# Masked attention scores in 64x32 instead of 64x64 tiles of the PE array

## The reference, cut to what matters

```
bq = q.reshape(b, h, w, WINDOW, d) * QK_SCALE          # 8 heads of 64, WINDOW = 64
bk, bv = (look_around(bk), look_around(bv))            # the window before and the window itself: 128 keys
sim = jnp.einsum('bhwid,bhwjd->bhwij', bq, bk)
mask = (i < j) | (i > j + WINDOW) | (j == -1)
sim = jnp.where(mask, -jnp.finfo(sim.dtype).max, sim)
attn = jax.nn.softmax(sim, axis=-1)
out = jnp.einsum('bhwij,bhwjd->bhwid', attn, bv)
```

## Time and profile before

| | |
|---|---|
| three executions, us | 430.07, 433.26, 432.17 (median 432.17) |
| profiled execution, us from first to last instruction | 428.4; its own device time is not listed apart, and the three lie 1.7 to 4.9 above it |
| PE busy | 406.9 us (95%) in 4851 matmuls |
| DVE, ACT, POOL busy | 339.0, 306.0, 289.0 us |
| local attention, first layer | about 90 to 222 us, second about 259 to 391 us |
| mean granted clock of PE | 0.998 |

### The profile page before, as it was taken

One profiled execution on the slowest core, in us unless ns is written; L12 is line 12 of the kernel. 1 busy time (PEld: TensorE's weight loads), 2 busy tenths in 40 slices (PEclk: granted clock), 3 DMA queues, 4 the chain that ended last, 5 costly groups with the idle time before them and its releaser, 6 DMA issues. The chain is left out here.

```text
span 428.4 us, 13218 instructions
## 1 busy us (share of the span) xinstructions
PE 406.9 (95%) x4851; PEld 290.3 (68%) x4851; DVE 339.0 (79%) x717; ACT 306.0 (71%) x690; POOL 289.0 (67%) x284
## 2 busy tenths in 40 slices
PE   5989999899999999999999999999999999999994
PEld 2667666557777777777776566677778777766563
DVE  4787777899798899899754376898899899855676
ACT  3868777777688878887873247688878878876324
POOL 2576799899778778777714346677777767761425
PEclk9999999999999999999999999999999999999999
DMA  7840000000000000000000000000000000000012
GB/s 194 311 98 2 4 3 3 2 1 2 13 10 9 12 10 8 8 16 8 6 8 15 0 2 3 8 8 8 12 10 8 11 12 8 7 10 13 7 37 63
DMA packets 21054, 10.37 MB, mean 24 GB/s; under 512 B 13252, under 2 KB 20224, under 8 KB 20992
## 3 DMA queue, kind: packets, MB, share of 16 engines
q1 hardware_dynamic: 20384, 9.32, 8.0%
q10 hardware_dynamic: 608, 0.21, 0.2%
HBM read 6.38 MB, written 1.05 MB: 17 GB/s over the span
## 5 line engine op out<-in xcount | busy, mean ns | idle before, releaser
L461 POOL TENSOR_TENSOR qr<-rot 128x1024 f32<-128x1024 f32 x32 | 75.8, 2370 | 28.1 <-DVE rot L2071 23.4
L659 PE MATMUL psum<-wqkv_sb,h_t 128*128 128x512 f32 x192 | 93.2, 595 | 1.0 <-issue 0.8
L469 POOL TENSOR_TENSOR qr<-qr,inv 128x1024 f32<-128x1024 f32 x32 | 60.8, 1901 | 34.3 <-ACT inv L1422 34.3
L2079 DVE TENSOR_REDUCE ss<-sq 128x16 f32<-128x1024 f32 x32 | 39.0, 1218 | 13.6 <-ACT sq L1411 13.6
L2099 DVE TENSOR_REDUCE neg_max<-psum 128x4 f32<-128x512 f32 x64 | 41.5, 685 | 6.3 <-PE psum L659 4.8
L1436 ACT ACTIVATE probs<-probs 128x512 f32<-128x512 f32 x62 | 38.2, 631 | 9.6 <-DVE probs L2106 9.4
L659 PE MATMUL psum<-z_t,w_sb 128*128 128x512 f32 (+1 forms) x96 | 44.7, 595 | 0.0
L659 PEld LDWEIGHTS psum<-wqkv_sb,h_t 128*128 128x128 f32 x192 | 31.6, 191 | 18.2 <-issue 18.2
L2071 DVE TENSOR_TENSOR rot<-psum,cos_t 128x1024 f32<-128x1024 f32 x32 | 39.2, 1224 | 2.7 <-PE psum L659 2.4
L920 PEld LDWEIGHTS psum<-consts,qr 128*128 128x128 f32 x256 | 29.6, 141 | 16.7 <-POOL qr L469 12.8
L1382 ACT ACTIVATE gelu<-psum,columns 128x512 f32<-128x512 f32 (+1 forms) x24 | 16.5, 686 | 33.6 <-PE psum L659 33.5
(11 more groups left out here) (157 smaller groups left out, 964.3 us busy)
## 6 DMA issues: line engine op xcount, KB each, us to landing
wqkv_sb<-in_L_ffn_wqkv SPq DMA_DIRECT2D x1, 1536.0 KB, 9.8
hcat<-middle SPq DMA_DIRECT2D x32, 32.0 KB
hcat<-middle SPq DMA_DIRECT2D x32, 31.8 KB
out_x<-pong SPq DMA_DIRECT2D x7, 128.0 KB, 1.8
x_in<-in_L_attn_x SPq DMA_DIRECT2D x2, 384.0 KB, 4.3
w_sb<-in_L_ffn_w SPq DMA_DIRECT2D x1, 682.0 KB
cos_base<-rotary_cos SPq DMA_DIRECT2D x1, 512.0 KB, 5.2
sin_base<-rotary_sin SPq DMA_DIRECT2D x1, 512.0 KB, 6.4
```

The source lines that it names most:

```text
L461: pool.tensor_tensor(o, a, b[:, :, ::-1, :], ALU.add).then_inc(s["add_ready"], 1)
L469: pool.tensor_tensor(a, a, inv[:, :].unsqueeze(2).to_broadcast([P, 2 * AH, DH]), ALU.mult).then_inc(s["qr_ready"], 1)
L659: return pe.matmul(o, w, m, start=start, stop=stop, skip_group_check=skip)
L2079: dve.tensor_reduce(ss[:, 0:4 * AH:2], sq[:, :].rearrange("p (h e) -> p h e", e=DH), AX.X, ALU.add).then_inc(s["ss_ready"], 1)
```

## The change

The four mask products become eight of 32 output rows each (32 queries; a 64x32 piece of the array), in the order of the query blocks `i` first and the halves `a` second. The score products are cut by blocks of 32 queries as well, and each multiplies only the 96 keys that are not masked for all of its queries; where these lie in two windows they are two products. The columns left out keep the mask's -1e30. A tile has then 48 score products instead of 16 (32 in the first tile of each batch in each layer, which has no window before it). The semaphore is still incremented by the last one.

```
--- before.py
+++ after.py
@@ -929,28 +929,29 @@
                     wait(pe, s["qkt_ready"], N + 1)
                     wait(pe, s["pt0_ready"], N)
                     wait(pe, s["pt1_ready"], N)
-                    for a in range(2):
-                        r = slice(a * W, (a + 1) * W)
-                        for w in range(2):
-                            m = 1 if w else (2 if n < B else 0)
+                    Q = W // 2
+                    for i in range(2 * W // Q):
+                        w = i * Q // W
+                        m = 1 if w else (2 if n < B else 0)
+                        for a in range(2):
+                            r = slice(a * W, (a + 1) * W)
                             mask = masks_bf[r, m * P:(m + 1) * P].unsqueeze(1).to_broadcast([W, PAIRS, P])
-                            mm(p_sc[w * W:(w + 1) * W, a * 512:(a + 1) * 512].rearrange("p (c k) -> p c k", c=PAIRS),
-                               ident_bf[r, r], mask, start=True, stop=False, skip=True)
-                    slot, prev = n % 3 * 2 * INNER, (n - B if n >= B else n) % 3 * 2 * INNER
-                    blocks = qk_t[:, :].rearrange("p (t k) -> p t k", k=W)
+                            at = a * W + i * Q - w * W
+                            mm(p_sc[i * Q:(i + 1) * Q, a * 512:(a + 1) * 512].rearrange("p (c k) -> p c k", c=PAIRS),
+                               ident_bf[r, at:at + Q], mask, start=True, stop=False, skip=True)
+                    slot, prev = n % 3 * 2 * INNER, (n - B) % 3 * 2 * INNER
+
+                    parts = [(0, slot, 0, Q), (1, slot, 0, 2 * Q), (2, slot, 0, 3 * Q), (3, slot, Q, 4 * Q)]
+                    if n >= B:
+                        parts = [(0, prev, 2 * Q, 4 * Q), (1, slot, 0, 2 * Q), (2, slot, 0, 3 * Q), (3, slot, Q, 4 * Q),
+                                         (0, slot, 0, Q), (1, prev, 3 * Q, 4 * Q)]
                     for c in range(PAIRS):
-                        own = (slot + INNER + c * P) // W
-                        step = (prev + INNER + c * P) // W + 1 - own
-                        for w in range(2):
+                        for i, of, lo, hi in parts:
                             for a in range(2):
                                 r = slice(a * DH, (a + 1) * DH)
-                                k = blocks[r, own:own + step + 1:step] if step > 0 else blocks[r, own:own + step - 1:step]
-                                if w == 1:
-                                    k = blocks[r, own:own + 2]
-                                o = p_sc[w * W:(w + 1) * W, a * 512 + c * P:a * 512 + (c + 1) * P]
-                                q = slot + c * P + w * W
-                                ins = mm(o.rearrange("p (t k) -> p t k", k=W), qk_t[r, q:q + W], k,
-                                         start=False, stop=True, skip=True)
+                                k, q = of + INNER + c * P, slot + c * P + i * Q
+                                ins = mm(p_sc[i * Q:(i + 1) * Q, a * 512 + c * P + lo:a * 512 + c * P + hi],
+                                         qk_t[r, q:q + Q], qk_t[r, k + lo:k + hi], start=False, stop=True, skip=True)
                     ins.then_inc(s["sc_done"], 1)
 
                 def transpose_probs(n, par):
```

## The result

| | before | after |
|---|---|---|
| executions, us | 430.07 to 433.26 (4) | 440.89, 441.14, 440.89, 442.28 |
| median, us | 431.45 | 441.01 |
| ratio, 95% interval | | 1.0219 [1.0169, 1.0269] |
| profiled execution, span (own time) | 428.4 | 438.8 (440.89) |

A forecast was written before the change was run, and what follows sets the result against it. A ring from `o_n` through PE, ACT and DVE, without scores, was taken to set the 8.35 us tile; only four tiles gain, 4 x 0.10 = 0.4 us off the median of 432.17, giving 431.8 us, range 429.7 to 434.9.

The forecast's parts named there:

- The ring: Settled attention tiles: a chain from `o_n` through PE, ACT and DVE, without scores, sets 8.35 us; gain there 0.
- the slack of 0.03: Settled tiles: PE waits about 0.03 us for `o_n` at L987, its own work being 8.32 of 8.35 us.
- Masks: Start of a tile's block: eight mask matmuls side by side take 0.24 us, as the four did.
- Scores, by the array: Score matmuls: 768 columns a piece instead of 1,024, 0.66 us instead of 0.88, at most 0.22 saved a tile.
- Scores, by the number of instructions: Masks and scores: 104 matmuls instead of 36; bounds -0.22 and +1.0 us a tile, taken as -0.10.
- The rival: First mask to L893: 104 starts become the bound beyond 11 ns each, 2.7 us per further ns; 12%.
- the near row: Profile row of 32 matmuls of 64 columns in 64x32 pieces: 7.4 ns a start, 0.77 us for 104.
- Its 38 us: Estimated total loss if starts are never closer than about 25 ns; no more than 1% chance.
- More instructions to fetch: Whole kernel: 4,096 more PE instructions, 17 added packets, 0.28 MB; costed at nothing, 20 us without cover.
- The cover: PE instruction fetch: a packet's worth lasts PE some 8 us, which hides the fetch of a packet.
- Where scores are waited for: Tiles 2 and 3 of the first layer and the last tile of each layer: -0.10 us each, 0.4 in all.
- The forecast case: Whole kernel: time within 1% of before, about 4.3 us; 82%.

The follow-up runs named there:

- all keys: The changed kernel with each 32 queries multiplied with the 128 keys of the kernel before, 32 products a tile instead of 48: 432.98 us, ratio 1.0029.
- masks alone: The kernel before with the eight masks of 32 queries and its own 16 score products: 434.28 us, ratio 1.0089.

## Why the prediction was wrong

**The ring: right.** Half the products gave 1.3 us and a tile of 8.35. Also the slack of 0.03 was right: a block longer by 0.08 (all keys) makes a tile of 8.40, one longer by 0.16 (masks alone) a tile of 8.48, each time 0.03 less than the block grew by.

**Masks: right.** 0.23 from first mask to first score with eight abreast, for 0.24.

**Scores, by the array: a bound that was not reached.** The 0.22 were counted as if only the columns set the time. In the tiles with 32 products, where the longest piece has its 96 columns for each pair, the block is 0.10 shorter (1.11). That the forecast's 1.1 is met there is luck: it was made for 104 starts, with a discount for them, and these blocks have 72.

**Scores, by the number of instructions: this step failed.** It took -0.10 us a block; measured is +0.24 in tile 9 and +0.22 on average. It stayed near the short burst of 32 matmuls at 7.4 ns, though it wrote itself that such a burst may ride on a queue filled beforehand. The 104 did not keep that pace; whether a queue is the reason no run shows. Over 104 starts it is (0.23 + 1.27 - 0.20) / 103 = 12.6 ns, with 0.20 the mean of the last one's form. The rival had set its point at 11 ns and 2.7 us for each further one: 1.6 x 2.7 = 4.3 us, and the longer blocks cost 4. Place, point and price of the rival were right, and it got 12% because the near row was all but taken for a sustained rate. The measured pace lies between the two rows, 7.4 and 20 ns, and so did the point of 11 at which the rival begins.

The Trainium skill's rule that the prediction set beside it ("TensorE: Matmul & The Clock Gate", section "Wait — 56ns, not 53.3ns?"), no two starts closer than about 25 ns, is not borne out for starts on different pieces: 96 of them at 10.4 ns each with half the columns. Its 38 us did not come. But taken as a warning that starts have a floor whatever the columns, it pointed the right way.

**More instructions to fetch: this step failed too.** The cover was wrong: "a packet's worth lasts PE some 8 us" is a mean. In the block, 104 loads and 104 matmuls pass in 1.3 us, four fifths of a packet, so a packet that begins just ahead of the block (at 185.88, the block at 186.24) arrives when PE has already run out. The average hid the one place where it matters. That the pauses, 0.80 to 1.33, look like the prediction's price of 1.2 us for a packet without cover is luck: the 1.2 are a packet's transfer alone, while a pause is what is left uncovered of the transfer and the 1.2 to 1.6 us behind it. In the kernel with 64 products it went up to 2.4. The trace of before already had such a place, in the recurrent stage, PE alone:

```profile
22.57 0.34 PE L659 MATMUL psum<-hid,probs 64*32 64x64 f32 x14 [0.44 <-ACT probs L1326]
23.45 0.38 PE L659 MATMUL psum<-hid,probs 64*32 64x64 f32 x18 [0.53 <-issue]
```

A dense run of 32 stops after 14 for 0.75 us, 17 times 256 instructions ahead of the changed kernel's first pause in the same count, and goes on 1.45 after the end of a packet. All thirteen kernels have it (0.74 to 1.57), so it is no part of the comparison, but it was the row to cost the fetch from. Of the 16 packets added, it is not the number that costs: 49 packets with 32 products made no further pause. The Trainium skill says ("Runtime: NRT & Kernel Launch", section "Instruction fetch mechanics") that instructions come in blocks of 256, fetched while the block before them is executed, and that crossing a boundary is mostly hidden. The trace agrees on the size and, for the kernel before, on the hiding at all boundaries but that one; in the dense block a boundary cost up to 1.33 us.

**Where scores are waited for** gave nothing back, since the blocks there grew: tile 2 took 8.99 instead of 8.78.

The forecast case needed both failed steps to hold. With the rival's 4 us alone the time would have been 436; the pauses, which no rival had, make the rest.

What stays open: whether the load or the matmul sets the pace of the starts (each product here brings both); why it is 10 to 13 ns and not the same in all blocks (7 ns for the added ones), so that a start has no fixed price here; why eight pieces take 0.08 longer than four with the same columns; and why a packet begins now soon, now late behind the boundary before. A version that beats both kernels did not come out of this: half of the products, left out, were worth 1.3 us.

## What to carry to other kernels

A product cut into smaller pieces saves columns but multiplies loads and matmuls. A short burst of starts is no sustained rate: where the point at which the starts would lead (11 ns here) lies between the burst and the longest run in the trace (7.4 and 20), the loss deserves a greater chance than the 12% given here. And set the time that 256 instructions last at the densest place, not in the mean of a tile, beside a packet's way from the boundary before to its first instruction (3.25 to 3.68 us in four of the five pauses here, 5.27 in the last). Before that, ask whether the stretch is on the ring that sets the step: here even half of the products was worth only 1.3 of 431 us.

## What the runs showed of the hardware

- Instructions of PE came in packets of 16.4 KB, 0.9 to 1.6 us each. The pauses came only at places a multiple of 256 instructions apart, lasted up to 2.4 us, and ended 1.20 to 1.62 us after the packet's end; where PE reached such a place 1.9 us or more after the packet's end it did not stop. 64 instructions more at the program's start moved the pauses from tiles 6 and 11 to 3, 8 and 13.
- The first matmul in another shape of the array's tiles came 0.10 to 0.12 us later than in the same shape (64x64 behind 64x32, and 64x32 behind 64x64). The Trainium skill ("TensorEngine Tiling (Array Packing)", section "Key Properties") says that a change of the tiling mode drains the engine. The delay fits that, and would be its price here; the drain itself no trace shows.
- 96 matmuls with their 96 loads in 64x32 tiles took 1.07 us from first to last start, and still 0.99 with half of the columns: in such a run half of the columns counts for 0.08.
